# Six channel mixing runs moved into the last three bodies of a merged loop, and a gating product moved from VectorE to GpSimd

## The chip, the core and the metric

One Trainium2 chip, one core of it. The metric is the device time of one execution in microseconds; the numbers of this document are medians of repeated executions, and one further execution was recorded by the profiler.

## The reference

Two layers over x of shape 64 x 64 x 256 (64 sequences of 64 tokens, 256 channels), all in fp32. The first layer is a transformer layer: self attention, cross attention and an MLP with gelu. The second is an RWKV block: time mixing (token shift, a low rank mixer, a recurrence over the 64 tokens with an 8 x 8 state for each of 32 heads, a group norm, a gate) and then channel mixing. The lines that matter here are the end of time mixing and the whole of channel mixing:

```python
g = jax.nn.silu(xg @ Wg.T)
...
og = ((og - m) / jnp.sqrt(va + 1e-05)).reshape(b, l, e) * gn_w + gn_b
x1 = x + og * g @ Wo.T
xc = _ln(x1, ln2_w, ln2_b)
sx2 = jnp.concatenate([state[:, 0:1] - xc[:, :1], xc[:, :-1] - xc[:, 1:]], axis=1)
xk2 = xc + sx2 * ffn_maa_k
xr2 = xc + sx2 * ffn_maa_r
rr = jax.nn.sigmoid(xr2 @ Wfr.T)
kk = jnp.square(jax.nn.relu(xk2 @ Wfk.T))
return x1 + rr * (kk @ Wfv.T)
```

## The kernel before

The 4096 tokens are 16 **runs** of 256 tokens (`RUNS`, 2 tiles of 128). After the attention comes a merged loop, `bodies`, written as a software pipeline: body s does the scan of time mixing of run s, and beside it the mixing projections of run s+1, the first layer norm of run s+2, the MLP of run s+3 and the tail of time mixing (heads summed, group norm, gate, output projection, residual) of runs s-1 and s-2. Each engine has its own program for a body, written out by hand in a fixed order; engines meet by counting semaphores only, so a wait at the head of an engine's program holds all that stands behind it. A body is divided into eight groups n = 0 to 7 of the scan (`GROUPS_R`). On TensorE each group begins with `spread` (four transposes that put the values in PSUM), on VectorE with `scan` (a product from PSUM, then the scan instruction) and `read` (times the receptance; groups 2 and 3 of `read` are on GpSimd). Bodies 4 to 11 stand in a hardware loop; bodies -2 to 3 and 12 to 15 are unrolled.

The MLP reads run s+3, so it ends with body 12. In bodies 13, 14 and 15 TensorE has instead `keep_busy`: four matmuls into the MLP's bank `mlp`, whose result nobody reads, in groups 2 to 6 of bodies 13 and 14 and in groups 2 and 3 of body 15.

The group norm's output is transposed (`transpose_on`), scaled and shifted by `copy_on` on ScalarE (`onT`), multiplied by the gate in `apply_gate` (VectorE, after `scan(s, u, 0)` of the body two later; it signals `y_ready`), and `project_out` on TensorE multiplies it by `WoT`. The residual, `add_residual`, and the statistics, `make_stats`, follow on VectorE.

Channel mixing of run r goes through: `ch_normalise` (ScalarE), `ch_transpose` (TensorE, 4 transposes), `ch_copy_in` (ScalarE), `ch_shift` (GpSimd), `ch_mix` (VectorE, four instructions over 128 x 256), `ch_keys` (TensorE, 4 matmuls), relu and square (ScalarE), `ch_receptances` (4 matmuls), tanh (ScalarE), `ch_values` (4 matmuls), `ch_finish` (VectorE, two instructions over 128 x 512), and a store. It uses four PSUM banks, one for each of the four TensorE steps: `mlp`, `proj` and the two banks of `spread`. Two of these banks belong to the scan, so that channel mixing proper begins when the scans end: body 15 holds the first transposes, keys and receptances of run 0, and the 16 runs follow after the loop. The inverse deviations for it come in two parts (`NORMS`): runs 0 to 12, and 13 to 15.

## Time and profile before

| | |
|---|---|
| median of 3 runs | 1218.46 us (1216.35 to 1220.77) |
| the profiled execution | 1220.55 us, of which the profiler's span is 1218.8 us |
| TensorE busy | 1150.0 us (94%) |
| VectorE busy | 963.7 us (79%) |
| ScalarE busy | 776.8 us (64%) |
| GpSimd busy | 589.9 us (48%) |

How to read it: the span is the time from the first to the last instruction on the core. The median is 2.1 us under the profiled execution's time. The busy shares are averages over the attention, the merged loop (from about 510 us) and channel mixing (from about 1110 us), which have different limits. PE is TensorE, DVE is VectorE, ACT is ScalarE, POOL is GpSimd.

### The profile page before, as it was taken

Reading aid. Unit: us, or ns where it says so; the run is one execution under the profiler, and the core shown is the slowest. Engines: PE = TensorE matmul, PEld = TensorE weight load, DVE = VectorE, ACT = ScalarE, POOL = GpSimd, SP = SyncE. Lnnn points to the kernel's source line nnn. Section 1 sums busy time; section 2 is a strip of 40 time slices with the busy share of each in tenths; the row PEclk is TensorE's granted clock in tenths of the full one; section 3 lists DMA queues with packets and bytes.
Section 4 is the critical chain, followed back from the end, with each engine's and each line's share of the span. In section 5 each row is a group of like instructions: output and inputs, shape, how many; then the busy total and the mean of one; then the engine's idle time right before and its main releaser. Section 6 shows DMA issues by size and latency. Waiting matters only on the chain.

```text
span 1218.8 us, 35799 instructions
## 1 busy us (share of the span) xinstructions
PE 1150.0 (94%) x13664; PEld 978.5 (80%) x13664; DVE 963.7 (79%) x1670; ACT 776.8 (64%) x1750; POOL 589.9 (48%) x520
## 2 busy tenths in 40 slices
PE   5899999999999998999999999999999999886898
PEld 5888988889899876787788877888778887665787
DVE  5987778797777842389999999999999999897554
ACT  4778877778778754655576555665566653455664
POOL 4777788777887730343434434244342443331121
PEclk9999999999999989999999999999999999997999
DMA  9400000111111100000000000000000000000011
GB/s 332 129 3 1 0 1 3 29 38 46 44 39 39 36 2 1 1 1 1 2 1 1 1 1 1 0 0 0 0 0 0 0 2 1 1 1 1 36 52 52
DMA packets 25535, 27.31 MB, mean 22 GB/s; under 512 B 2336, under 2 KB 20064, under 8 KB 25056
## 3 DMA queue, kind: packets, MB, share of 16 engines
q1 hardware_dynamic: 25440, 25.99, 6.4%
q8 instruction: 65, 1.06, 0.4%
q14 instruction: 30, 0.25, 0.1%
HBM read 21.79 MB, written 4.19 MB: 21 GB/s over the span
## 4 chain that ended last, share of the span: by engine, by line
PE 72%; DVE 14%; issue 10%; POOL 2%; ACT 1%; DMA 0%; DVEq 0%; ACTq 0%; POOLq 0%
PE psum L934 9%; PE psum L353 9%; PE psum L943 7%; PE psum L267 5%; PE psum L336 4%; PE psum L1023 4%; PE psum L368 4%; PE psum L1060 4%; PE psum L297 3%; PE psum L280 3%; DVE shared L1663 3%; PE psum L1104 2%; DVE shared L1657 2%; PE psum L310 2%; PE psum L983 2%
## 5 line engine op out<-in xcount | busy, mean ns | idle before, releaser
L1663 DVE TENSOR_TENSOR_SCAN shared<-late_wT,shared 128x512 f32<-128x512 f32 x128 | 184.9, 1444 | 4.4
L849 POOL TENSOR_TENSOR late_xm<-late_mixed,late_xa 128x512 f32<-128x512 f32 x80 | 93.7, 1180 | 157.6 <-DVE late_mixed L1631 151.2
L232 POOL TENSOR_TENSOR shared<-shared,att_row_max 128x512 f32<-128x512 f32 x128 | 132.5, 1054 | 17.8 <-DVE att_row_max L564 17.8
L858 POOL TENSOR_TENSOR shared<-shared,late_rT 128x512 f32<-128x512 f32 x32 | 40.8, 1274 | 180.9 <-DVE shared L1663 180.9
L353 PE MATMUL psum<-shared 128*128 128x128 f32 x1024 | 127.4, 279 | 1.0 <-ACT shared L462 1.0
L453 ACT ACTIVATE shared<-shared 128x512 f32<-128x512 f32 x128 | 80.5, 631 | 69.6 <-POOL shared L232 69.5
L943 PE MATMUL psum<-w,late_hT 128*128 128x256 f32 x512 | 122.1, 383 | 1.0 <-ACT late_hT L1306 0.9
L353 PEld LDWEIGHTS psum<-shared 128*128 128x128 f32 x1024 | 121.5, 195 | 1.4 <-ACT shared L462 1.4
L1657 DVE TENSOR_TENSOR shared<-psum,shared 128x504 f32<-128x504 f32 x128 | 86.8, 678 | 43.5 <-PE psum L1060 42.2
L934 PE MATMUL psum<-late_glnT,w 128*128 128x256 f32 x512 | 118.4, 385 | 1.8 <-ACT late_glnT L1297 1.8
L564 DVE TENSOR_REDUCE att_row_max<-shared 128x8 f32<-128x512 f32 x128 | 86.8, 680 | 40.4 <-POOL shared L225 40.4
L943 PEld LDWEIGHTS psum<-w,late_hT 128*128 128x128 f32 x512 | 95.0, 190 | 18.7 <-issue 5.5
L934 PEld LDWEIGHTS psum<-late_glnT,w 128*128 128x128 f32 x512 | 96.1, 193 | 14.9 <-ACT late_glnT L1297 2.4
L1306 ACT ACTIVATE late_hT<-psum,cols 128x256 f32<-128x256 f32 x128 | 53.6, 470 | 77.8 <-PE psum L934 77.8
L225 POOL TENSOR_TENSOR shared<-shared 128x512 f32<-128x512 f32 x64 | 80.0, 1272 | 39.8 <-DVE shared L557 38.2
L225 POOL TENSOR_TENSOR shared<-shared,self_bias 128x512 f32<-128x512 f32 x64 | 80.2, 1276 | 31.1 <-DVE shared L557 31.1
L1674 DVE TENSOR_TENSOR shared<-shared,late_rT 128x512 f32<-128x512 f32 x96 | 91.7, 955 | 2.8
L267 PEld LDWEIGHTS psum<-shared 64*64 64x64 f32 x4096 | 66.3, 136 | 21.0 <-issue 20.9
L1060 PE MATMUL psum<-ident,shared 128*128 128x128 f32 x512 | 79.2, 278 | 1.0 <-DVE shared L1657 1.0
L1060 PEld LDWEIGHTS psum<-ident,shared 128*128 128x128 f32 x512 | 61.0, 141 | 20.6 <-issue 12.2
L1631 DVE SCALAR_TENSOR_TENSOR late_mixed<-psum,cols,late_sx 128x256 f32<-128x256 f32 x160 | 67.8, 474 | 11.8 <-PE psum L983 8.3
L462 ACT ACTIVATE shared<-psum 128x512 f32<-128x512 f32 x128 | 68.3, 585 | 8.8 <-PE psum L280 8.8
(162 smaller groups left out, 2697.9 us busy)
## 6 DMA issues: line engine op xcount, KB each, us to landing
shared<-in_enc SPq DMA_DIRECT2D x64, 128.0 KB, 2.6
out<-x SPq DMA_DIRECT2D x16, 256.0 KB, 2.0
x<-in_x SPq DMA_DIRECT2D x7, 512.0 KB, 9.7
w<-in_w SPq DMA_DIRECT2D x2, 1024.0 KB, 17.1
shared<-in_cross_mask SPq DMA_DIRECT2D x1, 1024.0 KB, 12.0
shared<-in_w_qkv SPq DMA_DIRECT2D x1, 768.0 KB, 4.6
x<-in_x SPq DMA_DIRECT2D x2, 256.0 KB, 3.8
shared<-in_w_kv SPq DMA_DIRECT2D x1, 512.0 KB, 12.8
```

Source lines behind the costliest of these rows:

```text
L225: nc.gpsimd.tensor_tensor(zs, zs, bias.unsqueeze(1).to_broadcast([P, PAIRS, S]), ALU.add).then_inc(biased, 1)
L232: nc.gpsimd.tensor_tensor(zs, zs, peak.unsqueeze(2).to_broadcast([P, PAIRS, S]), ALU.subtract).then_inc(shifted, 1)
L267: last = nc.tensor.matmul(out_banks[e ^ b][rows, pair * 32:pair * 32 + HD + 1], zT[keys, pair, rows], values[keys, u, e ^ b, pair, :], sta ...
L353: last = nc.tensor.matmul(dst[:, half * P:(half + 1) * P], w[:, kb, c0 + half * P:c0 + (half + 1) * P], src[:, u % 2, kb, 0:P], start=(kb ...
L564: nc.vector.tensor_reduce(out=row_max[:, u % 2, half * PAIRS:(half + 1) * PAIRS], in_=z[:, u % 2, half, :].rearrange("p (h k) -> p h k", k=S),
L849: nc.gpsimd.tensor_tensor(xm[:, m % 2, :, :].rearrange("p h (b t) -> p (h b) t", t=S), mixed[:, m % 2, :, :].rearrange("p h (b t) -> p (h ...
L934: last = nc.tensor.matmul(bank[:, (h % 2) * RT:(h % 2 + 1) * RT], w["w1"][:, kb, h * P:(h + 1) * P], glnT[:, kb, :], start=(kb == 0), stop ...
L943: last = nc.tensor.matmul(mlp[:, c * C:(c + 1) * C], hT[:, h, c * P:(c + 1) * P], w["w2"][:, h, :], start=(h == 0), stop=(h == HIDDEN - 1))
L1060: last = nc.tensor.transpose(v_banks[n % 2][:, a:a + P], v_rep[:, c, j0 + jj, half * P:(half + 1) * P], core.ident[:, :])
L1657: nc.vector.tensor_tensor(st[:, n, :, :, 1:S], v_banks[n % 2].rearrange("p (j b t) -> p j b t", j=JG, t=S)[:, :, :, 0:S - 1], kT[:, u, hal ...
L1663: nc.vector.tensor_tensor_scan(states, wT[:, u, half, :, :, :].rearrange("p j b t -> p (j b t)"), states, 0.0, ALU.mult, ALU.add).then_inc ...
L1674: nc.vector.tensor_tensor(states, states, rT[:, u, half, :].unsqueeze(1).to_broadcast([P, JG, RT]), ALU.mult).then_inc(read_ready, 1)
```

## The change

`keep_busy` is gone. Channel mixing of runs 0 and 1 stands in body 13, of runs 2 and 3 in body 14, of runs 4 and 5 in body 15 (`EARLY = 6`), spread over the groups of the scan. For these six runs all four TensorE steps write the one bank `mlp`, so that each step waits until the step before it has been read out of the bank. The tail after the loop has ten runs instead of sixteen, and is unrolled (before, the middle of it was a hardware loop). The early runs' squares and receptances lie where the MLP's first weight matrix was. The deviations come in three parts (runs 0 to 9, 10 to 12, 13 to 15), the first in body 12. In bodies 13 to 15 `add_bonus` stands in group 1 instead of 2, and two `repeat_values` stand later on ScalarE. `apply_gate` goes to GpSimd in all sixteen uses, as the second instruction of its body; its factor 0.5 goes into the group norm's scale and shift (`half_gn`, two tiny instructions before the loop).

```diff
-TAIL = 4
+EARLY = 6
+        def ch_bank(stage, r):
+            if stage == "tr" and r in (EARLY, EARLY + 1):
+                return (proj, v_banks[1])[r - EARLY]
+            if stage == "tr":
+                return mlp
+            return mlp if r < EARLY else {"key": proj, "recept": v_banks[0], "value": v_banks[1]}[stage]
-        NORMS = ((0, (RUNS - 3) * CH), ((RUNS - 3) * CH, RUNS * CH))
+        NORMS = ((0, (RUNS - 6) * CH), ((RUNS - 6) * CH, (RUNS - 3) * CH), ((RUNS - 3) * CH, RUNS * CH))
+        def early(s):
+            return isinstance(s, int) and s >= RUNS - 3
+        def early_run(s, i):
+            return CH * (s - (RUNS - 3)) + i
...
 gpsimd
+            def apply_gate(r, u):
+                pool.wait_ge(gate_done, r + 1)
+                pool.wait_ge(onT_copied, r + 1)
+                if later(r):
+                    pool.wait_ge(out_ready, r)
+                nc.gpsimd.tensor_tensor(yT[:, :], onT[:, :], gates[:, u, :], ALU.mult).then_inc(y_ready, 1)
             def body(s, u):
                 if there(s):
                     make_bonus(s, u)
+                if there(s - 2):
+                    apply_gate(s - 2, u)
                 if there(s + 1):
                     step_back(s + 1)
                 for n in range(GROUPS_R):
+                    if n == 2 and early(s):
+                        ch_shift(early_run(s, 0), 0)
...
+                    if n == 3 and early(s):
+                        ch_shift(early_run(s, 1), 1)
...
 tensor
-                    if isinstance(s, int) and s >= RUNS - 3 and 2 <= n < (4 if s == RUNS - 1 else 7):
-                        keep_busy(s)
+                        if early(s - 1):
+                            ch_values(early_run(s - 1, 1), 1)
+                        if early(s):
+                            ch_transpose(early_run(s, 0), 0)
+                        if early(s):
+                            ch_transpose(early_run(s, 1), 1)
+                    if n == 4 and early(s):
+                        ch_keys(early_run(s, 0), 0)
+                    if n == 4 and early(s):
+                        ch_receptances(early_run(s, 0), 0)
+                    if n == 5 and early(s):
+                        ch_values(early_run(s, 0), 0)
+                        if early(s):
+                            ch_keys(early_run(s, 1), 1)
+                    if n == 7 and early(s):
+                        ch_receptances(early_run(s, 1), 1)
...
             def ch_keys(r, u):
                 pe.wait_ge(ch_mixed_ready, r + 1)
-                if not later(r):
-                    pe.wait_ge(gate_done, RUNS)
+                if r < EARLY and r % 2 == 0:
+                    pe.wait_ge(ch_xc_ready, r + 2)
+                elif r < EARLY:
+                    pe.wait_ge(ch_rv_ready, r)
...
 vector
-            def apply_gate(r, u):
...
+                        if early(s - 1):
+                            ch_finish(early_run(s - 1, 1), 1)
+                    if n == (1 if early(s) else 2) and there(s):
+                        add_bonus(s, u)
...
+                        if early(s):
+                            ch_mix(early_run(s, 0), 0)
...
+                        if early(s):
+                            ch_mix(early_run(s, 1), 1)
...
+                        if early(s):
+                            ch_finish(early_run(s, 0), 0)
```

Three places show what stands in a row before and after. The first is TensorE in body 14, groups 2 to 4, before. L1060 is `spread`, L1113 `keep_busy`, L983 the mixer's pair, L1085 `transpose_o`, L1004 the decay's first projection, L1075 the sums over heads.

```order
L1060 MATMUL psum<-ident,shared 128x128 x4
L1113 MATMUL psum<-late_glnT,w1 128x256 x4
L983 MATMUL psum<-late_mixer_a,maa_w2a 128x256 x4
L1060 MATMUL psum<-ident,shared 128x128 x4
L1113 MATMUL psum<-late_glnT,w1 128x256 x4
L1085 MATMUL psum<-ident,shared 128x128 x4
L1060 MATMUL psum<-ident,shared 128x128 x4
L1113 MATMUL psum<-late_glnT,w1 128x256 x4
L983 MATMUL psum<-late_mixer_a,maa_w2a 128x256 x4
L1004 MATMUL psum<-late_xm,td_w1 64x128 x4
L1075 MATMUL psum<-shared,head_sum 32x256 x8
```

The same place after. L1083 is `spread`, L1006 the mixer's pair, L1222 `ch_transpose` of run 3, L1108 `transpose_o`, L1238 `ch_keys` of run 2, L1027 the decay's projection, L1098 the sums over heads, L1252 `ch_receptances` of run 2.

```order
L1083 MATMUL psum<-ident,shared 128x128 x4
L1006 MATMUL psum<-late_mixer_a,maa_w2a 128x256 x4
L1222 MATMUL psum<-ident,shared 128x128 x4
L1083 MATMUL psum<-ident,shared 128x128 x4
L1108 MATMUL psum<-ident,shared 128x128 x4
L1083 MATMUL psum<-ident,shared 128x128 x4
L1238 MATMUL psum<-late_hT,WfkT 128x256 x4
L1006 MATMUL psum<-late_mixer_a,maa_w2a 128x256 x4
L1027 MATMUL psum<-late_xm,td_w1 64x128 x4
L1098 MATMUL psum<-shared,head_sum 32x256 x8
L1252 MATMUL psum<-WfrT,late_hT 128x256 x4
```

Matmuls that waited for nothing have given way to matmuls of the same shape that wait for the other engines. The second place is VectorE in groups 4 and 5 of body 14, before: L1657 and L1663 are `scan`, L1674 `read`, L1691 to L1700 `centre`, L1631 `mix`, L1710 `sum_squares`; the six small rows of the deviations that stand between `read` and `centre` are left out at the "...".

```order
L1657 TENSOR_TENSOR shared<-psum,shared 128x8x63
L1663 SCALAR_TENSOR_TENSOR shared<-late_wT,shared 128x512
L1674 TENSOR_TENSOR shared<-shared,late_rT 128x512
...
L1691 TENSOR_TENSOR psum<-psum,shared 128x512
L1693 TENSOR_REDUCE late_mean<-psum 128x64
L1700 SCALAR_TENSOR_TENSOR shared<-late_mean,psum 128x256 x2
L1631 SCALAR_TENSOR_TENSOR late_mixed<-psum,cols,late_sx 128x256 x2
L1657 TENSOR_TENSOR shared<-psum,shared 128x8x63
L1663 SCALAR_TENSOR_TENSOR shared<-late_wT,shared 128x512
L1674 TENSOR_TENSOR shared<-shared,late_rT 128x512
L1631 SCALAR_TENSOR_TENSOR late_mixed<-psum,cols,late_sx 128x256 x2
L1710 TENSOR_REDUCE late_moments<-shared 128x64
```

And after, the same from `centre` on: L1768 to L1777 are `centre`, L1708 `mix`, L1835 `ch_mix` of run 3, L1734 to L1751 `scan` and `read`, L1843 and L1847 `ch_finish` of run 2, L1787 `sum_squares`.

```order
L1768 TENSOR_TENSOR psum<-psum,shared 128x512
L1770 TENSOR_REDUCE late_mean<-psum 128x64
L1777 SCALAR_TENSOR_TENSOR shared<-late_mean,psum 128x256 x2
L1708 SCALAR_TENSOR_TENSOR late_mixed<-psum,cols,late_sx 128x256 x2
L1835 SCALAR_TENSOR_TENSOR late_hT<-shared,cols 128x256 x4
L1734 TENSOR_TENSOR shared<-psum,shared 128x8x63
L1740 SCALAR_TENSOR_TENSOR shared<-late_wT,shared 128x512
L1751 TENSOR_TENSOR shared<-shared,late_rT 128x512
L1708 SCALAR_TENSOR_TENSOR late_mixed<-psum,cols,late_sx 128x256 x2
L1843 SCALAR_TENSOR_TENSOR w1<-w1,psum 128x512
L1847 SCALAR_TENSOR_TENSOR x<-w1,x 128x512
L1787 TENSOR_REDUCE late_moments<-shared 128x64
```

Six instructions have come between the scans here, and the next `scan` and `sum_squares` stand behind them. The third place is GpSimd in body 14 after: L849 is `make_bonus`, L874 `apply_gate`, L840 `step_back`, L912 `ch_shift`, L866 `read`, L857 `mix`, L881 `scale`.

```order
L849 TENSOR_TENSOR shared<-late_rT,shared 128x512
L874 TENSOR_TENSOR shared<-shared 128x512
L840 TENSOR_TENSOR late_sx<-late_xa 128x512
L912 TENSOR_TENSOR shared<-shared 128x512
L866 TENSOR_TENSOR shared<-shared,late_rT 128x512 x2
L857 TENSOR_TENSOR late_xm<-late_mixed,late_xa 128x512
L912 TENSOR_TENSOR shared<-shared 128x512
L857 TENSOR_TENSOR late_xm<-late_mixed,late_xa 128x512 x4
L881 TENSOR_TENSOR shared<-shared,late_rstd 128x512
```

Before, the rows L874 and L912 were not there; `apply_gate` now stands between `make_bonus` and `step_back` in every body from 2 on, `ch_shift` only in the last three.

## Rows read from the trace of the kernel before

**Rows 1.** The page: span, and part 1 (busy time, share, instructions).
```profile
span 1218.8 us, 35799 instructions
...
PE 1150.0 (94%) x13664; PEld 978.5 (80%) x13664; DVE 963.7 (79%) x1670; ACT 776.8 (64%) x1750; POOL 589.9 (48%) x520
```

**Rows 2.** Windows, two bodies of the loop: length, busy by engine, clock, DMA.
```profile
929.70:968.10 38.40, 37.58 (x245) 31.05 (x244) 35.88 (x52) 23.13 (x51) 14.79 (x11) 1.00 0.00 0
```

**Rows 3.** Windows: bodies 13, 14, 15, then the tail's steady part.
```profile
1006.50:1044.50 38.00, 33.32 (x217) 27.14 (x217) 35.46 (x52) 17.86 (x39) 12.85 (x11) 0.97 0.00 1
1044.50:1081.30 36.80, 32.24 (x215) 26.04 (x214) 33.70 (x52) 16.67 (x37) 12.50 (x11) 0.98 0.00 1
1081.30:1111.90 30.60, 19.88 (x126) 15.26 (x125) 29.15 (x41) 14.50 (x29) 8.11 (x6) 0.81 0.00 1
...
1162.70:1218.80 56.10, 52.00 (x257) 45.62 (x255) 26.50 (x53) 31.21 (x66) 8.32 (x8) 1.00 0.14 52
```

**Rows 4.** PE's timeline at a body's start in the loop: start, length, instructions.
```profile
933.61 1.99 PE L1104 MATMUL psum<-WoT,shared 128*128 128x256 f32 x8 [0.62 <-DVE shared L1718]
...
935.87 1.03 PE L961 MATMUL psum<-late_xin,maa_w 128*128 128x256 f32 x4
```

**Rows 5.** DVE's timeline at the same place.
```profile
930.32 1.81 DVE L1663 TENSOR_TENSOR_SCAN shared<-late_wT,shared 128x512 f32<-128x512 f32 x1
932.05 1.50 DVE L1718 SCALAR_TENSOR_TENSOR shared<-shared 128x512 f32<-128x512 f32 x1
...
934.68 0.86 DVE L1621 SCALAR_TENSOR_TENSOR late_xin<-late_sx,cols,late_xa 128x256 f32<-128x256 f32 x2
```

**Rows 6.** POOL's timeline there.
```profile
929.76 1.28 POOL L841 TENSOR_TENSOR shared<-late_rT,shared 128x512 f32<-128x512 f32 x1 [1.54 <-ACT late_rT L1353]
931.97 1.04 POOL L832 TENSOR_TENSOR late_sx<-late_xa 128x512 f32<-128x512 f32 x1 [0.92 <-ACT late_xa L1332]
```

**Rows 7.** Waits in the loop: who for whom, total, times, longest.
```profile
PE psum L1104 <- DVE shared L1718: 6.1, 10, 0.6
```

**Rows 8.** Lines from 1002 us on: count, busy, mean ns, idle before.
```profile
L1113 PE MATMUL psum<-late_glnT,w 128*128 128x256 f32 x96 | 22.7, 380 | 0.0
...
L892 POOL TENSOR_TENSOR shared<-shared 128x512 f32<-128x512 f32 x16 | 17.1, 1072 | 75.3 <-ACT shared L1453 75.3
```

**Rows 9.** DVE's timeline, bodies 13 and 14: where it was idle.
```profile
1043.92 0.68 DVE L1657 TENSOR_TENSOR shared<-psum,shared 128x504 f32<-128x504 f32 x1 [1.14 <-PE psum L1060]
...
1058.05 0.68 DVE L1657 TENSOR_TENSOR shared<-psum,shared 128x504 f32<-128x504 f32 x1 [1.90 <-PE psum L1060]
```

**Rows 10.** DVE's timeline, body 15: its start, sum of squares, first mix.
```profile
1081.22 0.67 DVE L1657 TENSOR_TENSOR shared<-psum,shared 128x504 f32<-128x504 f32 x1
...
1100.68 1.00 DVE L1710 TENSOR_REDUCE late_moments<-shared 128x64 f32<-128x512 f32 x1
...
1105.90 2.43 DVE L1765 SCALAR_TENSOR_TENSOR late_hT<-shared,cols 128x256 f32<-128x256 f32 x4 [0.93 <-POOL shared L892]
```

**Rows 11.** PE's timeline: run 0's keys, a run of the steady tail, the last matmuls.
```profile
1108.39 3.78 PE L1202 MATMUL psum<-late_hT,WfkT 128*128 128x256 f32 x8 [2.80 <-DVE late_hT L1765]
...
1162.68 0.60 PE L1190 MATMUL psum<-ident,shared 128*128 128x128 f32 x4
1163.11 1.89 PE L1202 MATMUL psum<-late_hT,WfkT 128*128 128x256 f32 x8
...
1168.30 0.60 PE L1190 MATMUL psum<-ident,shared 128*128 128x128 f32 x4
...
1212.81 1.89 PE L1227 MATMUL psum<-WfvT,shared 128*128 128x256 f32 x8
```

**Rows 12.** DVE's timeline, one run of the steady tail.
```profile
1165.92 1.67 DVE L1765 SCALAR_TENSOR_TENSOR late_hT<-shared,cols 128x256 f32<-128x256 f32 x4 [3.19 <-POOL shared L892]
1167.51 0.68 DVE L1773 SCALAR_TENSOR_TENSOR shared<-shared,psum 128x512 f32<-128x512 f32 x1
1168.35 0.69 DVE L1777 SCALAR_TENSOR_TENSOR x<-shared,x 128x512 f32 x1 [0.16 <-DVE shared L1773]
```

More of the change, by code:

```diff
@@ L781, in norm_of @@
         def norm_of(r):
-            return 1 if isinstance(r, int) and r < RUNS - 3 else 2
+            return [2 * r < stop for _, stop in NORMS].index(True) + 1
         def s_is(s, value):
@@ L1106, in project_out @@
                 last.then_inc(out_ready, 1)
-            def keep_busy(s):
-                if s_is(s, RUNS - 3):
-                    pe.wait_ge(mlp_x, RUNS)
-                for h in range(2):
-                    for kb in range(HALVES):
-                        nc.tensor.matmul(mlp[:, h * RT:(h + 1) * RT], w["w1"][:, kb, h * P:(h + 1) * P], glnT[:, kb, :],
-                                         start=(kb == 0), stop=(kb == HALVES - 1))
             def body(s, u):
@@ L1189, in ch_transpose @@
                         a = half * RT + c * P
-                        last = nc.tensor.transpose(ch_tr[:, a:a + P], ch_xn[:, u, c, half * P:(half + 1) * P],
+                        last = nc.tensor.transpose(ch_bank("tr", r)[:, a:a + P], ch_xn[:, u, c, half * P:(half + 1) * P],
                                                    core.ident[:, :])
@@ L1201, in ch_keys @@
                     for kb in range(HALVES):
-                        last = nc.tensor.matmul(ch_key[:, half * RT:(half + 1) * RT],
+                        last = nc.tensor.matmul(ch_bank("key", r)[:, half * RT:(half + 1) * RT],
                                                 w["WfkT"][:, kb, half * P:(half + 1) * P], ch_xk[:, u, kb, :],
@@ L1207, in ch_receptances @@
             def ch_receptances(r, u):
-                if not later(r):
+                if r < EARLY:
+                    pe.wait_ge(ch_relu_ready, r + 1)
+                elif r == EARLY:
                     pe.wait_ge(kv_ready, RUNS * GROUPS_R - 1)
@@ L1219, in ch_values @@
                 pe.wait_ge(ch_kk_ready, r + 1)
-                if not later(r):
-                    pe.wait_ge(kv_ready, RUNS * GROUPS_R)
+                if r < EARLY:
+                    pe.wait_ge(ch_rr_ready, r + 1)
+                elif r == EARLY:
+                    pe.wait_ge(ch_xc_ready, EARLY + 2)
                 else:
@@ L1482, in body @@
                     copy(s, u, NG)
-                if there(s):
+                if s_is(s, RUNS - 3):
+                    ch_normalise(0, 0)
+                    ch_normalise(1, 1)
+                if there(s) and not early(s):
                     repeat_values(s, u, 2)
@@ L1489, in body @@
                     mixer(s + 1)
+                if early(s):
+                    ch_copy_in(early_run(s, 0), 0)
                 if there(s - 1):
@@ L1524, in body @@
                     make_decays(s + 1, 1 - u)
+                if early(s) and s < RUNS - 1:
+                    ch_square(early_run(s, 1), 1)
+                if there(s + 1):
                     repeat_values(s + 1, 1 - u, 1)
@@ L1542, in body @@
                     copy_in(s + 2)
+                if early(s) and s < RUNS - 1:
+                    ch_normalise(early_run(s + 1, 0), 0)
+                    ch_normalise(early_run(s + 1, 1), 1)
             def s_inverts(s):
@@ L1592, in prepare @@
                 last.then_inc(u_ready, 1)
+                for i, name in enumerate(("gn_w", "gn_b")):
+                    c0 = COLS[name][0]
+                    last = nc.vector.tensor_scalar(half_gn[:, i, :], core.cols[:, c0:c0 + HALVES], 0.5, None, ALU.mult)
+                last.then_inc(half_set, 1)
             attention_residual, divide, spreads, variances, shifts = att.vector(dve, prepare)
@@ L1757, in ch_mix @@
                 dve.wait_ge(ch_sx_ready, r + 1)
-                if not later(r):
+                if r == 0:
                     dve.wait_ge(down_ready, RUNS)
@@ L1780, in channel @@
             def channel(s, u):
-                if later(s):
-                    ch_finish(s - 1, 1 - u)
+                ch_finish(s - 1, 1 - u)
                 if there(s + 2):
@@ L1791, in body @@
                         scan(s, u, n)
-                    if n == 0 and there(s - 2):
-                        apply_gate(s - 2, u)
+                    if s_is(s, RUNS - 3) and n == 0:
+                        ch_shifts(0)
                     if there(s):
@@ L1803, in body @@
                     if n == 2:
-                        if there(s):
-                            add_bonus(s, u)
                         if there(s - 2):
@@ L1833, in body @@
                         mix(s + 1, 4)
+                    if n == 7 and s_is(s, RUNS - 1):
+                        ch_mix(EARLY, 0)
             end = TILES - 1
```

168 lines of the change are left out of this document (91 added, 77 removed).

## The prediction

> **What bounds the kernel now.** I read the page first [rows 1]: TensorE is busy 94% of a span of 1218.8 us. An average over stages says little here, so I then cut the end of the span into windows, one per body. In the loop a pair of bodies takes 38.4 us each, with TensorE busy 37.58 and VectorE 35.88 [rows 2]: TensorE sets the pace, VectorE is 2.5 us behind. In bodies 13 and 14 the two change places: TensorE 33.32 of 38.00 and 32.24 of 36.80, VectorE 35.46 and 33.70 [rows 3]. And in TensorE's figure are the unread matmuls: L1113 has 96 records, two to a matmul, so 48 matmuls or 12 calls, 22.7 us in all [rows 8]. Start to start four matmuls of this shape take 1.73 us (1163.11 to 1164.84 in the timeline; the run of 5.62 us from 1162.68 to 1168.30 is 0.44 of transposes and three times 1.73) [rows 11]. So of TensorE's time in bodies 13 and 14 five calls, 8.7 us each, are filler. In the steady tail TensorE is again the limit: 52.00 of 56.10, clock 1.00, VectorE at 26.50 [rows 3]. The reader is to see: TensorE binds before body 13 and after the loop, VectorE in between.
>
> **The tail.** I anchor it at the end of `sum_squares` of run 14, 1100.68 + 1.00 = 1101.7 [rows 10], since GpSimd's `scale`, the last transpose and the gate of run 14 all follow from it. From there to the end are 117.1 us. TensorE has 14 transposes and 16 of each of the three matmul steps of channel mixing left there, 14 x 0.44 + 48 x 1.73 = 89.2 us, about 6.3 of time mixing (two output projections of 1.73, the heads' sums, transposes), and 4.3 after the last matmul's start-to-start time (1212.81 + 1.73 to 1218.8) [rows 1, 11]: 99.8, so 17.3 us are waits and slow clock. One is in the rows: the keys of run 0 waited 2.80 us and took 3.78 instead of 1.89 for their records [rows 11], and the window of body 15 has the clock at 0.81, so part of it at the lower level, 1.2 GHz, after TensorE had been idle for a third of it [rows 3]. Changed: 9 transposes, 10 keys, 11 receptances, 11 values are left at that point, 9 x 0.44 + 32 x 1.73 = 59.3, with the same 6.3 and 4.3, 69.9 us. The waits: ScalarE must invert the deviations, load a table, copy in run 6 and square run 5 before TensorE gets run 5's receptances, and the gate of run 14 stands behind their tanh on ScalarE, so I keep 15 of the 17.3. That gives 85, against 117.1: **-32**. Bounds of the waits: 10 (the chain is hidden) to 20 (it is longer), so -37 to -27.
>
> **Bodies 13 to 15.** Each early run adds on VectorE `ch_mix`, 1.67, and `ch_finish`, 0.68 + 0.69 [rows 12]; the removed gate is 0.66 when nothing disturbs it and 1.50 in the loop [rows 5], where most of it is waiting. On TensorE body 13 gets 0.88 + 5 x 1.73 = 9.5 for 8.7 of filler, body 14 11.3 for 8.7: it could carry that in its idle time. On VectorE body 13 gets two mixes and one finish, 4.7, less 0.7 of gate: +4.0; body 14 two of each less the gate and the deviations' 1.0 that go: +4.4. VectorE was idle 1.14 and 1.90 at its largest gaps [rows 9], but those gaps stand where it waits for `spread` on TensorE, and only some of them fill. Besides, GpSimd gets three more instructions a body (two shifts at 1.07 [rows 8], the gate). Those collide with VectorE: 1.50 instead of 0.66 for the gate just while GpSimd ran `step_back` from 931.97 to 933.01 [rows 5, 6], 2.43 instead of 1.67 for the first `ch_mix` [rows 10, 12]. I take 0.5 per added instruction, 1.5 a body (bounds 0 and 3 x 0.84). Following the order of each engine through body 13 with these durations, VectorE stays the late one: `ch_mix` of run 1 pushes scan 5, and `ch_finish` of run 0 comes before the sum of squares; TensorE waits about 5 us for the mixer's last product and 1 us for run 1's keys, whose bank `ch_finish` must have read. Body 13: +4.0 + 1.5 less 0.9 of filled gaps, **+4.6**. Body 14: +4.4 + 1.5 less 1.8, **+4.1**. Body 15 has no gap to fill: 29.15 busy of 30.60 [rows 3]. From its start to the anchor (1081.22 to 1101.7 [rows 10]) it gets two mixes, two finishes, the second deviations (1.0), less the gate: 3.3 + 2.7 + 1.0 - 0.7 = 6.3, and 1.5 of collisions, **+7.8**. Sum +16.5; bounds +5 (the additions of bodies 13 and 14 vanish in gaps, no collisions) and +28 (below, third rival). What hides the matmuls of the early runs is VectorE's own length; if VectorE were quicker, their 9.5 and 11.3 us would have to fit beside 33.32 - 8.7 = 24.6 us of other work on TensorE, and they would.
>
> **The gate on GpSimd, in the loop.** The output projection waits for the gate on VectorE: 0.62 us [rows 4], 6.1 us over 10 bodies [rows 7]. No row shows this product on GpSimd; the nearest are GpSimd's over the same shape, 1.04 and 1.28 [rows 6], so 1.2. `make_bonus` ends at 931.04 and copied input is there by then; the scan that waited for GpSimd goes first and ends at 932.1 [rows 5], the gate then ends near 933.1 instead of 933.55, and `step_back` behind it near 934.4 instead of 933.0. VectorE's `read` and the mixer's input (934.68 to 935.54 before) have 0.7 less in front of them but now wait for `step_back`: they end near 935.4. TensorE starts the projection 0.5 earlier, and the mixer (935.87 before [rows 4]), which waits for that input, 0.4 earlier. What is late next is the mixer's input. 12 bodies (2 to 13) x 0.4 = **-4.5**; bounds: -7 (the whole 0.62, with body 13's) and +4 (the input 0.3 later each).
>
> The Trainium skill, "SBUF — State Buffer", section "Who interferes with whom", says that a VectorE instruction with two SBUF inputs and a GpSimd instruction that reads SBUF exclude each other, the loser blocking entirely. By that rule the trace agrees: 1.50 against 0.66 above; it speaks against this part of the change, since a 1.2 us holder replaces a 0.66 us one, and taken alone it would turn the term of -4.5 into 12 x (1.2 - 0.66) = +6.5, an estimate.
>
> **The small edits** I cost at nothing: `half_gn` runs before the loop beside TensorE-bound attention; `add_bonus` and `repeat_values` change places within a body with 2 to 4 us to spare (if not, under 1 us); ScalarE is busy 17.86 of 38.00 and gets 31.21 / 10 = 3.1 us for each run, 6 a body [rows 3]; the deviations' instructions lie between table loads that are there already, and VectorE's 1.0 us of them in body 12 has the 2.5 us of slack of a loop body [rows 2] (1 us if it hasn't).
>
> **Sum.** -32 + 16.5 - 4.5 = -20.0. Against its own time of 1220.55 that is 1200.6; against the median, 2.1 lower, **1198.5**.
>
> **Rivals.**
> 1. VectorE absorbs the additions (15%): gaps of 1.14 and 1.90 and more [rows 9] take bodies 13 and 14 whole, growth +5 to +8 instead of 16.5: 1187 to 1190. For: TensorE has room. Against: 33 to 35 us busy already in 37.
> 2. The gate in the loop is a wash or a loss (15%): `step_back` behind it makes the mixer's input 0 to 0.5 later; term 0 to +6, so 1203 to 1209. For: the collisions in rows 5 and 6. Against: the projection's 0.62 is freed in any case, and the residual add needs no SBUF pair. The rule of the Trainium skill's page "SBUF — State Buffer" would give 1209.5, at this rival's far end.
> 3. One bank makes a chain (12%): transposes, keys, receptances, values of two runs, each waiting for ScalarE or VectorE to read the bank, at fixed places of TensorE's order. If each of five hand-overs a body costs TensorE 1 us more that VectorE then also waits for (through `spread`), +28 instead of 16.5: 1210. For: `ch_keys` of the second run waits for a `ch_finish` behind scan 5. Against: between two uses stand 2 to 6 us of other work.
> 4. The other side (4%): the gate on GpSimd holds `step_back` behind a scan too, 1.3 us of gate plus 1.26 of scan, so that every body's mixer starts later. It decides from 15.5 / 12 = 1.3 us a body; at 2.0 the time is 1227. Against: the scan would have to win the pair twice.
> 5. The change makes no difference (2%): only if growth eats the tail's gain.
>
> The forecast itself has 52%, own range 1193 to 1204. The range 1188 to 1209 leaves out part of 1, the far half of 3, and 4. 0.3%, or 3.7 us, is about what a measurement of this kernel tells from no change: faster 0.93, same 0.03, slower 0.04.
>
> **What would show it.** Right: no wait of the projection for the gate in the loop, a body near 38.0 us, a wait of the mixer for VectorE's input in its place; bodies 13 and 14 near 42 and 41 with VectorE without gaps and TensorE waiting for `mix` before its last product; the gate's rows on GpSimd near 1.2; 85 us from the sum of squares of run 14 to the end. Wrong: bodies 13 and 14 at 37, or over 45 with VectorE idle before `spread`; or a loop body over 38.5.

## The result

| | median | runs | ratio [95% interval] |
|---|---|---|---|
| before | 1220.32 us (1216.35 to 1225.85) | 10 | |
| changed | 1210.77 us (1207.81 to 1215.96) | 10 | 0.9926 [0.9905, 0.9947] |

The change makes the kernel 9.6 us faster. The forecast was 20, and the time lies 12.3 us above the forecast and 1.8 us above the range; 1.9 of the 12.3 are the median of before, which was 1218.46 over three runs when the forecast was made. One execution among all that follow, of the version with half the early mixing left out, was a slow one of 1347.76 us: it counts in that version's median and not in its ratio. The profiled execution of the changed kernel has a span of 1209.0 us, that of before 1218.8 [rows 1], so the two traces differ by 9.8 us, about as the medians do.

The page's first part for the changed kernel, to be read against [rows 1]:

```profile
span 1209.0 us, 35528 instructions
PE 1136.9 (94%) x13568; PEld 962.8 (80%) x13568; DVE 962.4 (80%) x1663; ACT 777.5 (64%) x1752; POOL 630.1 (52%) x536
```

TensorE lost 13 us of busy time and GpSimd won 40 (16 gates, and the waiting inside its instructions); these totals say nothing of where the span went. For that I cut the end of the span at the same instructions in both traces: VectorE's first scan product of bodies 13, 14 and 15, and the end of `sum_squares` of run 14 (the anchor of the forecast).

| us | to body 13 | body 13 | body 14 | body 15 to anchor | anchor to end |
|---|---|---|---|---|---|
| before | 1006.15 | 37.77 | 37.30 | 20.46 | 117.12 |
| changed | 1006.64 | 43.84 | 44.03 | 30.36 | 84.13 |
| difference | +0.5 | +6.1 | +6.7 | +9.9 | -33.0 |
| forecast | -4.5 | +4.6 | +4.1 | +7.8 | -32 |

(One of the forecast's 12 bodies for the gate is body 13 itself; the term stands in the first column whole.) The tail came out near its forecast. The last bodies grew by 22.7 us instead of 16.5, and all that lies ahead of body 13 lost 0.5 where 4.5 were to be gained. The windows of the four stretches, of the changed kernel:

```profile
core 0: us, PE busy (x) PEld busy (x) DVE busy (x) ACT busy (x) POOL busy (x), PEclk, DMA share, GB/s
1006.64:1050.48 43.84, 37.27 (x228) 29.30 (x227) 41.28 (x61) 25.99 (x56) 18.88 (x14) 0.92 0.02 7
1050.48:1094.51 44.03, 37.65 (x230) 30.41 (x229) 40.55 (x57) 23.73 (x51) 18.53 (x14) 0.92 0.04 13
1094.51:1124.87 30.36, 22.33 (x135) 17.41 (x134) 28.27 (x46) 13.21 (x27) 8.42 (x6) 0.89 0.03 10
1124.87:1209.00 84.13, 70.58 (x346) 58.68 (x344) 45.18 (x88) 49.95 (x100) 16.63 (x14) 0.98 0.10 38
```

And those of before, cut at the same instructions (the windows of [rows 3] begin elsewhere):

```profile
core 0: us, PE busy (x) PEld busy (x) DVE busy (x) ACT busy (x) POOL busy (x), PEclk, DMA share, GB/s
1006.15:1043.92 37.77, 33.09 (x218) 26.73 (x217) 35.23 (x51) 18.06 (x40) 12.42 (x10) 0.98 0.00 1
1043.92:1081.22 37.30, 32.74 (x216) 26.54 (x215) 34.20 (x52) 16.72 (x38) 12.88 (x11) 0.97 0.00 1
1081.22:1101.68 20.46, 15.33 (x115) 11.76 (x112) 20.08 (x30) 10.47 (x21) 3.76 (x3) 0.97 0.00 1
```

Two columns matter. VectorE's busy time grew by 6.05, 6.35 and 8.19 us, where the forecast had 5.5, 5.9 and 7.8: 1.4 us too little in all. Its idle time (length less busy time) went from 2.54, 3.10 and 0.38 to 2.56, 3.48 and 2.09, so it grew by 2.1 us, where the forecast let 2.7 us of it fill: 4.8 us. These two make the 6.2. And the granted clock fell from 0.98, 0.97 and 0.97 to 0.92, 0.92 and 0.89. TensorE's timeline in body 13 shows what stands behind that number (start, duration, line, operation, idle time before it and who ended it):

```profile
1019.82 2.08 PE L1006 MATMUL psum<-late_mixer_a,maa_w2a 32*128 32x256 f32 x8 [2.76 <-DVE x L1794]
1021.83 1.11 PE L1222 MATMUL psum<-ident,shared 128*128 128x128 f32 x4
1022.74 1.06 PE L1083 MATMUL psum<-ident,shared 128*128 128x128 f32 x4
1023.59 1.06 PE L1108 MATMUL psum<-ident,shared 128*128 128x128 f32 x4
1024.45 1.06 PE L1083 MATMUL psum<-ident,shared 128*128 128x128 f32 x4
```

L1006 is the mixer's product `mix_pair`, L1083 `spread`. TensorE waits 2.76 us at `mix_pair` for the residual add on VectorE (in body 14 it is 3.06; body 15 has waits of 2.35, 2.83 and 4.14 at other places), and then works at 1.2 GHz: the four transposes of `spread` last 1.06 us, against 0.60 at the full clock (below). VectorE's scan product behind it then waits for `spread` 1.33 us in body 13 and 1.93 in body 14. VectorE's waits over the three bodies:

```profile
engine line waited for: us in total, times, longest us
DVE shared L1734 <- PE psum L1083: 4.0, 4, 1.9
DVE w L1843 <- PE psum L1267: 1.5, 1, 1.5
DVE late_xin L1698 <- POOL late_sx L840: 1.3, 2, 0.9
```

In the hardware loop, the same place as in [rows 4 to 6], and with it the gate of run 15 in the tail (L874 at 1133.59):

```profile
929.56 1.29 POOL L849 TENSOR_TENSOR shared<-late_rT,shared 128x512 f32<-128x512 f32 x1 [1.55 <-ACT late_rT L1394]
930.81 2.19 POOL L874 TENSOR_TENSOR shared<-shared 128x512 f32<-128x512 f32 x1
932.95 1.49 POOL L840 TENSOR_TENSOR late_sx<-late_xa 128x512 f32<-128x512 f32 x1
...
1133.59 1.27 POOL L874 TENSOR_TENSOR shared<-shared 128x512 f32<-128x512 f32 x1 [4.06 <-DVE late_hT L1835]
...
933.05 2.00 PE L1127 MATMUL psum<-WoT,shared 128*128 128x256 f32 x8 [0.27 <-POOL shared L874]
934.48 0.88 DVE L1698 SCALAR_TENSOR_TENSOR late_xin<-late_sx,cols,late_xa 128x256 f32<-128x256 f32 x2 [0.33 <-POOL late_sx L840]
935.41 1.13 PE L984 MATMUL psum<-late_xin,maa_w 128*128 128x256 f32 x4
```

The order of events is the forecast's: `make_bonus`, the gate until 933.0, `step_back` until 934.4, then the mixer's input and the mixer. But against the start of `make_bonus` in its own body the mixer begins 5.85 us in, before 6.11 (929.76 to 935.87 [rows 4, 6]): 0.26 earlier, not 0.4. And from one body to the next only 0.17 of it is left: ScalarE's gate tanh recurs every 38.26 us (before 38.43). Body 12 in turn takes 39.42 us by that measure, before 38.28, and body 1 39.13, before 37.50. Sum: the first body starts 0.4 earlier, bodies 2 to 11 gain 1.6, body 1 loses 1.6 and body 12 1.1, and 0.3 go off between ScalarE's mark and the cut of body 13: +0.5 with the decimals. Of the four stretches this one is the least sure. The version without the filler, below, has the instructions of before up to body 13 and got there at 1003.57, 2.6 us earlier; versions that have the changed kernel's up to there came at 1002.35 and at 1008.35. What repeats is the period: for bodies 5 to 10 it lies between 38.42 and 38.46 us in all four traces with the gate on VectorE, and between 38.25 and 38.29 in all nine with it on GpSimd. The tail is also less sure than the bodies: the four versions below whose instructions behind the anchor are the changed kernel's had 85.8, 85.9, 87.2 and 88.0 us where it had 84.1.

### The profile page after: what moved, and what is told of

It reads as the page before. It is cut to its first block, busy times and chain, and to the rows that moved or that the text cites. A ratio compares the mean times of both kernels' runs of the same rounds, so it can differ in the third digit from the quotient of the medians.

```text
span 1209.0 us, 35528 instructions
## 1 busy us (share of the span) xinstructions
PE 1136.9 (94%) x13568; PEld 962.8 (80%) x13568; DVE 962.4 (80%) x1663; ACT 777.5 (64%) x1752; POOL 630.1 (52%) x536
## 3 DMA queue, kind: packets, MB, share of 16 engines
q8 instruction: 65, 1.06, 0.4%
HBM read 21.79 MB, written 4.19 MB: 21 GB/s over the span
## 4 chain that ended last, share of the span: by engine, by line
PE 67%; DVE 12%; issue 12%; POOL 5%; ACT 3%; DMA 0%; POOLq 0%; DVEq 0%; ACTq 0%
PE psum L957 10%; PE psum L353 9%; PE psum L966 6%; PE psum L267 5%; PE psum L336 5%; PE psum L368 4%; PE psum L297 3%; PE psum L1046 3%; PE psum L280 3%; PE psum L1083 3%; DVE shared L1740 3%; POOL shared L874 2%; PE psum L310 2%; PE psum L1127 2%; PE psum L1006 2%
## 5 line engine op out<-in xcount | busy, mean ns | idle before, releaser
L857 POOL TENSOR_TENSOR late_xm<-late_mixed,late_xa 128x512 f32<-128x512 f32 x80 | 95.9, 1206 | 163.9 <-DVE late_mixed L1708 157.6
L1734 DVE TENSOR_TENSOR shared<-psum,shared 128x504 f32<-128x504 f32 x128 | 86.8, 678 | 41.7 <-PE psum L1083 39.6
L866 POOL TENSOR_TENSOR shared<-shared,late_rT 128x512 f32<-128x512 f32 x32 | 40.7, 1273 | 150.1 <-DVE shared L1740 150.1
L1751 DVE TENSOR_TENSOR shared<-shared,late_rT 128x512 f32<-128x512 f32 x96 | 103.2, 1075 | 4.0
L1083 PE MATMUL psum<-ident,shared 128*128 128x128 f32 x512 | 80.8, 282 | 0.1
L1708 DVE SCALAR_TENSOR_TENSOR late_mixed<-psum,cols,late_sx 128x256 f32<-128x256 f32 x160 | 67.8, 474 | 13.4 <-PE psum L1006 9.9
L1083 PEld LDWEIGHTS psum<-ident,shared 128*128 128x128 f32 x512 | 62.9, 144 | 19.0 <-issue 10.9
## 6 DMA issues: line engine op xcount, KB each, us to landing
shared<-in_w_kv SPq DMA_DIRECT2D x1, 512.0 KB, 12.3
```

The lines of the kernel that those rows point to most:

```text
L857: nc.gpsimd.tensor_tensor(xm[:, m % 2, :, :].rearrange("p h (b t) -> p (h b) t", t=S), mixed[:, m % 2, :, :].rearrange("p h (b t) -> p (h ...
L1083: last = nc.tensor.transpose(v_banks[n % 2][:, a:a + P], v_rep[:, c, j0 + jj, half * P:(half + 1) * P], core.ident[:, :])
L1734: nc.vector.tensor_tensor(st[:, n, :, :, 1:S], v_banks[n % 2].rearrange("p (j b t) -> p j b t", j=JG, t=S)[:, :, :, 0:S - 1], kT[:, u, hal ...
L1751: nc.vector.tensor_tensor(states, states, rT[:, u, half, :].unsqueeze(1).to_broadcast([P, JG, RT]), ALU.mult).then_inc(read_ready, 1)
```

## Experiments

The bodies are cut as above throughout, except body 12, whose length is the one between ScalarE's gate tanhs; a gain of body 12 by that measure can't be added to one of body 13 by the scans, since the two overlap. Each version has one trace. Of the times, most differences between versions of the changed kernel lie within overlapping intervals, so what a stretch costs is read from the traces. Theory A is the forecast's picture with one thing added: VectorE sets the pace of the last bodies, and the filler taken out of TensorE let its clock fall, which comes back to VectorE through `spread`. Theory B puts the loss on GpSimd, whose gate takes SBUF from VectorE. Later rivals stand in each expectation.

**The gate alone**, the kernel before with nothing but the gate moved (and `half_gn`):

```diff
 gpsimd, body
+    if there(s - 2):
+        apply_gate(s - 2, u)
     if there(s + 1):
         step_back(s + 1)
 vector, body
-    if n == 0 and there(s - 2):
-        apply_gate(s - 2, u)
```

> The kernel before, with only the gate moved to GpSimd (and its 0.5 put into the scale). Theory A (the mixer's input waits for step_back, so little of the projection's 0.62 us comes back): loop bodies of 38.27 us instead of 38.44, in all 2 us faster than before, ratio 0.998. Theory B (the gate gives the forecast 0.4 us a body, and the change lost it elsewhere): bodies of 38.0, 5 us faster, ratio 0.996. Theory C (the gate on GpSimd costs time in the unrolled bodies): slower than before.

Measured: 1219.92 us (12 runs) beside 1219.31 (23 runs), ratio 1.0001 [0.9989, 1.0014]. The loop body is 38.27, as Theory A has it. The trace reaches body 13 at 1003.0, which tells nothing (1003.57 in the next run, where no instruction up to there is changed), and of 2 us nothing is seen in the times. Bodies 13, 14 and 15 measured -0.7, +0.7 and +0.5. The interval allows 1.3 us of gain at most, less than either theory's: the gate by itself is worth nothing that can be measured.

**Without the filler**, the kernel before with `keep_busy` taken out and nothing in its place:

```diff
-    if isinstance(s, int) and s >= RUNS - 3 and 2 <= n < (4 if s == RUNS - 1 else 7):
-        keep_busy(s)
```

> The kernel before without its unread matmuls and nothing in their place. If TensorE's clock is what they bought (theory A), bodies 13 to 15 show stretches at the lower level after their waits, and scans that wait for spread: 2 to 6 us slower than before, ratio 1.002 to 1.005. If VectorE paces these bodies whatever the clock is (theory B): within 1 us of before, ratio 1.000.

Measured: 1222.76 us, 1.0026 [1.0012, 1.0040], by the ratio 3.2 us slower. The bodies grew by 0.6, 1.1 and 1.7 us, 3.4 in all. Their granted clock was 0.80, 0.80 and 0.77, where before has 0.98, 0.97 and 0.97. VectorE's waits for `spread` in bodies 13 to 15, before and then without the filler:

```profile
DVE shared L1657 <- PE psum L1060: 4.8, 5, 1.9
DVE shared L1655 <- PE psum L1060: 8.1, 7, 3.3
```

They grew by 3.3 us, nearly the whole. So the matmuls that nobody reads were worth 3 us: they held the clock. The forecast counted them as TensorE's time alone.

**The gate back on VectorE**, in the changed kernel:

```diff
 vector, body
+    if n == 0 and there(s - 2):
+        apply_gate(s - 2, u)
 gpsimd, body
-    if there(s - 2):
-        apply_gate(s - 2, u)
```

> The changed kernel with the gate back on VectorE. Theory A (VectorE is full in bodies 13 to 15 and the gate on GpSimd is worth 0.17 us a loop body): 2 us slower than the changed kernel from the loop, and 0 to 1 us either way in bodies 13 to 15. Theory B (the gate's collisions with VectorE in bodies 13 to 15 are what made them grow more than forecast): these three bodies take 3 us or more less than in the changed kernel, so that the whole is 1 us or more faster than it.

Measured: 1210.19 us, 0.9927 [0.9903, 0.9951], the same as the changed kernel's 0.9926. Bodies 13 to 15 were 1.5, 0.4 and 0 us shorter, the loop 1.6 longer and the tail 1.3 longer. Theory B asked for 3 us less in these bodies and falls: the gate on GpSimd isn't what made them long. The 1.9 us came with a clock of 0.96, 0.96 and 0.83 instead of 0.92, 0.92 and 0.89; the run with fillers and the gate back, below, tells the two apart.

**Fillers put back**: unread matmuls, four to a call, at five places where TensorE waits in bodies 13 to 15 (two calls at the last of them, so six calls), in banks free at that moment. One place stands for all:

```diff
+def keep_warm(bank):
+    for h in range(2):
+        for kb in range(HALVES):
+            nc.tensor.matmul(bank[:, h * RT:(h + 1) * RT], w["w2"][:, kb, h * P:(h + 1) * P], glnT[:, kb, :],
+                             start=(kb == 0), stop=(kb == HALVES - 1))
...
+    if early(s) and mixing:
+        pe.wait_ge(ch_xc_ready, early_run(s, 0) + 1)
+        keep_warm(mlp)
     if mixing:
         mix_pair(s + 1, 0)
```

> The changed kernel with five calls of unread matmuls put back where TensorE waits in bodies 13 to 15: one before the mixer's pair in bodies 13 and 14 (waits of 2.8 and 3.1 us), in body 15 one before run 13's transposes (2.4), one before run 4's keys (2.8), two before run 5's (4.1). Theory A (slow clock after those waits delays spread and run 3's values, and VectorE with them, by 1.3, 1.9 and 1.5 us): 3 to 5 us faster than the changed kernel, bodies 13 and 14 at 42.5 and 42, no row of 1.06 us for a spread in them. Theory B (VectorE's own load and collisions make the growth, the clock is hidden): within 1 us of the changed kernel.

Measured: 1207.5 us (4 runs), 0.9903 [0.9885, 0.9920]; bodies 42.39, 42.24 and 28.83, that is 1.45, 1.8 and 1.5 us shorter, 4.8 in all. TensorE at the place in body 13 shown above (L1134 is the filler, L1239 the transposes of run 0):

```profile
1016.16 1.99 PE L1134 MATMUL psum<-late_glnT,w 128*128 128x256 f32 x8
1019.03 1.13 PE L1006 MATMUL psum<-late_mixer_a,maa_w2a 32*128 32x256 f32 x8 [0.88 <-DVE x L1811]
1020.10 0.66 PE L1239 MATMUL psum<-ident,shared 128*128 128x128 f32 x4
1020.59 0.60 PE L1083 MATMUL psum<-ident,shared 128*128 128x128 f32 x4
```

The wait is 0.88 instead of 2.76, and `mix_pair` takes 1.13 instead of 2.08. The windows and VectorE's waits over the three bodies:

```profile
1005.85:1048.24 42.39, 36.47 (x236) 28.28 (x235) 41.16 (x61) 25.99 (x56) 18.86 (x14) 1.00 0.02 7
1048.24:1090.48 42.24, 38.42 (x247) 30.68 (x246) 40.58 (x58) 23.73 (x51) 18.55 (x14) 1.00 0.04 13
1090.48:1119.31 28.83, 26.14 (x162) 20.66 (x160) 28.25 (x46) 13.09 (x27) 8.72 (x6) 1.00 0.03 11
```

```profile
DVE late_xin L1715 <- POOL late_sx L840: 1.3, 2, 0.9
DVE shared L1751 <- PE psum L1083: 0.7, 2, 0.6
```

Clock 1.00 in all three, VectorE's busy time unchanged (41.16 against 41.28), and its waits for TensorE down from 4.0 + 1.5 to 0.7 us: 4.8 us, the whole of what the bodies gained. In the traces Theory A is shown, and it repeats: the three other versions with fillers and the gate on GpSimd, below, have 42.2 and 28.8 us for bodies 14 and 15 too. In the times the fillers are worth 3.3 us by the medians (1210.8 to 1207.5), with intervals that overlap, so that gain isn't shown. The tail became 1.7 us longer (85.79). In it TensorE waits 4.19 us for the relu of run 5, which stands on ScalarE behind the inversion of the last deviations and a table load, and the eight records of the receptances behind it take 3.63 us. In the changed kernel that wait is 1.95 and the records take 2.00.

**Body 12's deviations behind the mix**, one way to get back what body 12 lost:

```diff
-    if s_is(s, RUNS - 4) and n == 4:
-        ch_variances(0)
...
         mix(s + 1, 2)
+    if s_is(s, RUNS - 4):
+        ch_variances(0)
```

> The changed kernel with the first deviations of body 12 put behind the mixer's third product on VectorE instead of ahead of centring. Theory A (body 12 takes 39.42 us because TensorE's last mixing product waits for VectorE, which has 1.0 us of deviations in front of it): body 12 at 38.3 to 38.6, 1 us faster than the changed kernel. Theory B (it is ScalarE's added inversion in body 12 that delays the projection into the next body): body 12 stays at 39.4.

Measured: 1210.44 us beside 1221.08 (13 runs), 0.9917 [0.9891, 0.9944]. Body 12 went from 39.42 to 38.76, so these instructions cost 0.7 of the 1.1 us; the time as a whole didn't move beyond its interval. Bodies 13 and 14 were 1.2 us shorter each, at a clock of 0.96 and 0.95, and the tail 3.9 us longer (88.04); why the tail grew is taken up at the end of this section.

**Half of the early mixing left out:**

```diff
-    for half in range(HALVES):
+    for half in range(1 if r < EARLY else HALVES):
```

> The changed kernel, which leaves out half of the token mixing of the six early runs (2 of 4 VectorE instructions each, 0.8 us), so that their output isn't the reference's. Theory A (VectorE paces bodies 13 to 15): bodies 13 and 14 shorter by 1.0 to 1.6 us each (the first mix of each stands before a wait for spread), body 15 to the sum of squares by 1.6, in all 3 to 5 us. Theory B (the one bank's chain of hand-overs between TensorE and ScalarE paces them): under 1 us in all.

Measured: 1207.49 us, 0.988 [0.9846, 0.9915]; the bodies 0.8, 1.1 and 3.2 us shorter, 5.1 in all, for six times half of a `ch_mix` (0.84 each by [rows 12], 5.0). The sum agrees better than its parts. VectorE's busy time fell by 1.6, 1.5 and 1.7 us; its idle time grew by 0.8 and 0.4 in bodies 13 and 14 and fell by 1.5 in body 15, where the clock was 0.97 instead of 0.89.

**Half of the early values matmuls left out:**

```diff
-    for kb in range(HALVES):
+    for kb in range(1 if r < EARLY else HALVES):
         ... ch_kk[:, u, a:a + P], w["WfvT"][:, kb, :]
```

> The changed kernel, which leaves out half of the value matmuls of the six early runs (2 of 4 each, 0.86 us of TensorE), so that their output isn't the reference's. Theory A (TensorE's added work in bodies 13 to 15 is hidden behind VectorE): under 1.5 us in all, most of it in body 15, where VectorE waits 1.5 us for run 3's values. Theory B (the one bank's chain or TensorE paces them): 3 to 5 us.

Measured: 1212.02 us, 0.9937 [0.9915, 0.9960]; the bodies 0.1, 0.4 and 0.8 us shorter, 1.2 in all. The two runs say the same from both sides: over the three bodies work on VectorE is paid at about its full length (4.7 us of busy time, 5.1 of span), and work on TensorE is mostly hidden. These are readings of the traces: by the medians the second version isn't faster than the changed kernel at all. The one bank as a chain (rival 3) is not what was paid either: a values step half as long would then have shortened the chain by 0.87 us each time, 5.2 in all.

**Combined**: fillers, body 12's deviations late, and run 5's squared keys ahead of the inversion on ScalarE, against the 4.19 us wait at the head of the tail:

```diff
-    if early(s) and s < RUNS - 1:
+    if early(s):
         ch_square(early_run(s, 1), 1)
...
     ch_normalise(EARLY + 1, 1)
-    ch_square(EARLY - 1, 1)
```

> The changed kernel with the five calls of unread matmuls of the experiment on the clock, the first deviations of body 12 behind the mixer's third product, and run 5's relu and square ahead of the inversion of run 14's deviations on ScalarE. Theory A (the three losses are separate): 4.7 us in bodies 13 to 15, 1 us in body 12, and 1 to 4 us after the sum of squares, since TensorE there waits 4.2 us for that relu: 1202 us. Theory B (VectorE's own length at the end of body 15 sets when the tail starts): 1205 us, as the earlier square gives nothing.

Measured: 1207.76 us, 0.9895 [0.9864, 0.9926]; bodies 41.75, 42.24 and 28.82, body 12 at 38.75, tail 87.04. The bodies are those that were expected, but the time is neither theory's, and the tail is 1.3 us longer than with the fillers alone. The last three runs ask why.

**Fillers and the early square, without the late deviations:**

> The changed kernel with the five filler calls of the run with fillers, and with run 5's squared keys ahead of the inversion on ScalarE; the late deviations stay where the change has them. Theory A (the 1.2 GHz stretches were a price of the bodies, and ScalarE's order sets the first microseconds of the tail): bodies 42.4, 42.2 and 28.8 us, with granted clock 1.00, as with the fillers alone. The combined version had 87.0 us of tail, and TensorE read PE clock 0.75 and 0.66 in two stretches of it. If the late deviations made that tail, this one is 85.0 us (0.8 less than with fillers alone, 85.8), and the median 1206.5. Theory B (the 4 us wait of TensorE there is paid once whatever its order): tail 85.8 to 87, median 1207.5 to 1208.

Measured: 1205.52 us (4 runs) beside 1220.15 (11 runs), 0.9878 [0.9858, 0.9898]: the lowest median of all, 14.6 us under the kernel before, though its interval overlaps that of the fillers alone. Bodies 42.42, 42.23 and 28.81, as Theory A has them; the tail is 83.29, 1.7 less than Theory A's.

**Fillers, and the gate back on VectorE:**

> The changed kernel with the fillers, and the gated output back on VectorE. Theory A: what the gate on GpSimd costs in the last bodies (VectorE's collisions, 1.5 us in body 13 when the gate went back) and what the slow clock costs there are two separate prices, so the bodies are 40.9, 41.8 and 28.8 us, 1.9 less than with the fillers alone; the loop is 1.7 us longer, so the median is the same, 1207.3. Theory B: the 1.5 us in body 13 was the clock too (PE's half-clock stretch was shorter there), so with the fillers the bodies are 42.4, 42.2 and 28.8 as in the run with the gate on GpSimd, and the median is 1209.2.

Measured: 1210.34 us, 0.9923 [0.9906, 0.9939]; bodies 42.37, 43.61 and 28.72, tail 86.90. Body 13 is 42.37, as with the gate on GpSimd: so the 1.5 us that it gained when the gate went back were the clock, not SBUF (Theory B of this run). Body 14's 43.61 neither theory had; its clock is 0.96. Its median is 2.8 us above that with the fillers alone, but the two intervals of the ratio overlap ([0.9906, 0.9939] and [0.9885, 0.9920]); that the gate on GpSimd is worth something beside the fillers is not shown.

**Fillers and the late deviations, without the early square:**

> The changed kernel with the fillers, and body 12's deviations behind the mix. Against the combined version it lacks only the early squaring. Theory A (that the squaring first does nothing, since what it frees is given back at the half clock of TensorE behind the wait for the values of run 5): bodies 41.8, 42.2, 28.8, body 12 at 38.75, tail 85.8 to 87, median 1207.5. Theory B (squaring first cost time in the tail): tail 85.8 or less, median 1206.

Measured: 1207.62 us, 0.9906 [0.9889, 0.9924]; body 12 at 38.74, bodies 41.74, 42.24 and 28.83, tail 87.20. The numbers are Theory A's. Bodies 12 and 13 together, from scan to scan, took 80.77 us instead of 81.61 with the fillers alone, 0.8 less; the tail took 1.4 more, and the median stayed.

Where the tails part is one wait. Rows of TensorE's timeline in the version with fillers and early square, the combined one, and the one with fillers and late deviations (values matmuls, `ch_values`), in this order:

```profile
1128.54 1.97 PE L1284 MATMUL psum<-WfvT,w 128*128 128x256 f32 x8 [2.49 <-ACT w L1530]
1165.93 1.97 PE L1284 MATMUL psum<-WfvT,w 128*128 128x256 f32 x8 [1.94 <-DVE w L1859]
```

```profile
1124.69 3.75 PE L1284 MATMUL psum<-WfvT,w 128*128 128x256 f32 x8 [2.49 <-ACT w L1530]
1164.19 3.41 PE L1284 MATMUL psum<-WfvT,w 128*128 128x256 f32 x8 [1.93 <-DVE w L1859]
```

```profile
1164.74 3.23 PE L1284 MATMUL psum<-WfvT,w 128*128 128x256 f32 x8 [1.93 <-DVE w L1860]
```

The waits are the same to 0.01 us, 2.49 and 1.93, behind the same instructions of TensorE from the last scan on; in one execution the clock stays and the eight records take 1.97, in the others it falls and they take 3.2 to 3.8. At the second wait the next values matmuls come 7.13 us later with the clock held (1165.93 to 1173.06) and 8.82 without: 1.7 us. In the profiled executions it fell there in four (all three with late deviations, and the one with fillers and the gate back) and held in the changed kernel and five others. Each version with late deviations also had a longer tail than its twin without (88.0 and 84.1, 87.0 and 83.3, 87.2 and 85.8). Whether they bring it about, by what they shift, or whether it is chance, these runs don't tell; each version has one profile.

## Why the prediction was wrong

**The tail, -32**: right, though that it came within 1 us is in part luck. 84.1 us were measured for 85, and of the 17.3 us of waits and slow clock about 14 stayed, for the 15 taken; the same instructions took 85.8 to 88.0 in four other versions, all inside the bounds given (80 to 90). The wait of TensorE for ScalarE's inversion was there as described: 1.95 us in the changed kernel, behind keys that took 3.75 us at 1.2 GHz, and 4.19 with the fillers. Putting run 5's relu and square ahead of the inversion made the tail 2.5 us shorter in the traces where the clock held (85.79 to 83.29); the medians went from 1207.5 to 1205.5, with intervals that overlap.

**The last bodies, +16.5**: this is the step that failed, by 6.2 us. Its picture was right: VectorE stays the late one (half the mixing off: -5.1; half the values off: -1.2). The missing piece is the sentence on what hides the matmuls: TensorE "could carry that in its idle time". I took 48 unread matmuls from TensorE, which then was idle for 2.8, 3.1, 2.4, 2.8 and 4.1 us at a time, and costed everything behind at the full clock. The 0.81 of body 15 was in my rows [rows 3], and I used it for the tail and not here. Measured, the slow clock is 4.8 us of the 6.2 (fillers put back), and it is also what kept VectorE's gaps open where I let 2.7 us of them fill. The other 1.4 us are VectorE's busy time: the collisions with GpSimd cost some 0.5 us a body more than the 1.5 of the forecast (four of the six `ch_mix` took 2.31 to 2.59 us where [rows 12] has 1.67), if all of it is put down to them. Part of it is an instruction that the forecast's list lacks: the early runs' deviations end in one small product (`ch_shifts`), which took 0.17 us in body 15 before and takes 1.17 in body 13 now.

**The gate in the loop, -4.5**: the second step that was off, by 2.5 us (the rest of the first column's 5.0 is body 1, body 12 and that column's scatter). The mechanism is as told: the projection's wait fell from 0.62 to 0.27, VectorE now waits 0.33 for `step_back`, the gate takes 2.19 with waiting and 1.27 without (I took 1.2). But a body gained 0.17 and not 0.4, 1.6 us over bodies 2 to 11 and 2.0 over the forecast's twelve, and taken alone the product's move gave 1.0001 [0.9989, 1.0014]. I read the gain at one place of the body and took it for the gain of the period. Where the other 0.1 of the 0.26 goes isn't shown. Rival 2, a wash, was nearest to the truth. By the rule of the Trainium skill's page "SBUF — State Buffer", section "Who interferes with whom", the term would have been +6.5, an estimate of the forecast; the trace agrees with the rule's mechanism (2.19 against 1.27 us in one instruction) and not with that price: none of the three versions with the gate on GpSimd was measurably slower than its twin with the gate on VectorE.

**The small edits, nothing**: body 12's deviations were given 1 us "if it hasn't" the slack, and it hadn't: a loop body's 2.5 us of idle VectorE [rows 2] are not slack at that place. Body 12 lost 1.1 us, 0.7 of it by them; the rest stays open. Body 1's 1.6 us stand below.

**Range and rivals**: rival 1 (VectorE absorbs the additions) fell, the bodies grew by 22.7 us. Rival 3 named almost the measured time, 1210, but its chain isn't what the runs found. That it came near is luck. The range had no case in which the clock costs anything in bodies 13 to 15, and its upper end, the far end of rival 2, was 1.8 us short.

## What to carry to other kernels

Unread matmuls are not free time: before you replace them by real work, look at where TensorE will wait (2.4 to 4.1 us at a time here), and keep a filler there. When VectorE sets the pace, cost a TensorE edit not by its busy time alone but by what its clock does to the transposes VectorE waits for. And a gain at one place of a software pipeline counts only as far as the next body starts earlier; measure the period, not the place.

## What I had not expected of the hardware

The clock's fall is not settled by the wait alone. Behind equal waits at the same place (1.93 and 1.94, 2.49 and 2.49 us, above) it fell in one execution and held in another. Body 1 shows the same between before and changed, and nothing that the change moves stands in body 1. Windows of the changed kernel, and of before:

```profile
550.00:552.50 2.50, 1.71 (x7) 1.33 (x8) 2.47 (x5) 1.98 (x4) 0.00 (x0) 0.82 0.00 0
552.50:555.00 2.50, 2.50 (x24) 1.28 (x25) 2.00 (x3) 0.61 (x3) 0.00 (x0) 0.50 0.00 0
```

```profile
550.42:552.92 2.50, 1.72 (x10) 1.13 (x11) 2.47 (x5) 1.98 (x4) 0.00 (x0) 1.00 0.00 0
552.92:555.42 2.50, 2.50 (x32) 1.91 (x32) 2.40 (x4) 1.75 (x7) 0.00 (x0) 1.00 0.00 0
```

Up to there the two agree: in the 2.50 us ahead of these TensorE is busy 2.01 us with 16 records at clock 1.00 in both, and the wait for VectorE at their border is 1.21 us in both. Behind the wait the four records of the mixer's product take 1.92 us in one and 1.13 in the other, and TensorE goes on at 1.2 GHz in one and at 2.4 GHz in the other; the body takes 39.1 or 37.5 us by it. Of the thirteen profiled executions four had 39.1, of versions with the gate on GpSimd, and nine 37.5, five of them with it. So 1.6 us of the difference between the two traces lie in a place that the change doesn't touch. What decides whether the clock falls stays open.
